# Writing out the second edge loop of a two-layer graph network on one Trainium2 core

## The reference

```python
h = gelu(edge_scalar_attr @ W_mlp1 / sqrt(8));  h = gelu(h @ W_mlp2 / sqrt(64))
w00, w01, w10, w11 = h @ Wp_00, h @ Wp_01, h @ Wp_10, h @ Wp_11
e0, e1 = feat0[edge_src], feat1[edge_src]          # a gather of 128 floats per edge
mid0 = [w00 * e0 * ea0,  w11 * sum(e1 * ea1) / sqrt(3)]
mid1 = [(w01 * e0) * ea1, w10 * e1 * ea0]
n0, n1 = segment_sum(mid0, edge_dst), segment_sum(mid1, edge_dst)
```

## Time and profile before

| | us |
|---|---|
| runs of the kernel | 5851.09, 5867.39, 5890.79 (median 5867.39) |
| span of the profiled execution | 5855.7 |
| edge loop of the second layer, first gather to last accumulation | 3144 to 5792 |
| busy in the span | PE 3865.5 (66%), DVE 3222.6 (55%), POOL 3371.9 (58%), ACT 1837.0 (31%) |

### The profile page before, as it was taken

How to read it: one execution, slowest core, us unless ns; L and a number is a source line. 1 busy time by engine, 2 the same in 40 slices (tenths; PEclk the granted TensorE clock), 3 DMA queues, 4 the chain that set the end, 5 groups by cost and what they waited for, 6 DMA issues and landing times. The chain is left out here.

```text
span 5855.7 us, 86247 instructions
## 1 busy us (share of the span) xinstructions
PE 3865.5 (66%) x15016; PEld 2606.4 (45%) x15016; DVE 3222.6 (55%) x10018; ACT 1837.0 (31%) x5130; POOL 3371.9 (58%) x3264
## 2 busy tenths in 40 slices
PE   2666666666666666666664775786776677776676
PEld 2334444434444444444443554554554455454454
DVE  3344454545444554454554675675666556675665
ACT  1234334344334344334452221221222122222221
POOL 3455555555555555555525776666777666767763
PEclk6878878888888888888876897887888778887787
DMA  5433333333333333333311111111111111111111
GB/s 151 120 103 100 100 99 98 93 101 104 96 100 100 100 98 101 98 102 99 101 51 54 44 44 43 43 42 43 44 43 44 41 42 44 44 42 45 43 42 41
DMA packets 395313, 430.82 MB, mean 74 GB/s; under 512 B 195187, under 2 KB 286839, under 8 KB 394888
## 3 DMA queue, kind: packets, MB, share of 16 engines
q0 software_dynamic: 103168, 211.49, 13.8%
q1 hardware_dynamic: 291560, 216.64, 13.7%
q10 hardware_dynamic: 288, 0.04, 0.0%
HBM read 411.18 MB, written 16.65 MB: 73 GB/s over the span
## 5 line engine op out<-in xcount | busy, mean ns | idle before, releaser
L171 POOL DMA_INDIRECT ring_rows<-xl,ring_idx x1612 | 1537.0, 953 | 1444.3 <-DVE attn_msg L1043 898.6
L218 POOL DMA_INDIRECT ahead_rows<-feat,ahead_idx x1612 | 1796.1, 1114 | 834.1 <-issue 513.5
L878 PE MATMUL attn_sums_ps<-attn_msg,attn_onehot 128*128 128x136 f32 x3224 | 601.9, 344 | 934.8 <-DVE c_acc_attn L984 541.8
L1433 PE MATMUL conv_sums_ps<-conv_vals,conv_onehot 128*128 128x256 f32 x3224 | 924.6, 436 | 157.6 <-issue 95.9
L878 PEld LDWEIGHTS attn_sums_ps<-attn_msg,attn_onehot 128*128 128x128 f32 x3224 | 524.3, 240 | 987.6 <-DVE c_acc_attn L984 742.6
L1464 ACT ACTIVATE conv_scaled<-conv_w_ps,c_xT 128x64 f32<-128x64 f32 x1612 | 373.4, 314 | 1643.7 <-remote 729.0
L1433 PEld LDWEIGHTS conv_sums_ps<-conv_vals,conv_onehot 128*128 128x128 f32 x3224 | 654.5, 214 | 414.1 <-issue 310.1
L1440 PE MATMUL conv_w_ps<-c_Wp,conv_hid 128*128 128x256 f32 x1612 | 505.7, 444 | 484.1 <-ACT conv_hid L1470 266.5
L929 ACT ACTIVATE attn_fifth<-attn_pre_ps,c_b_r 128x512 f32<-128x512 f32 x403 | 275.0, 683 | 1505.4 <-remote 953.7
L1049 DVE SCALAR_TENSOR_TENSOR attn_leaky<-attn_pre_ps,c_b_r,attn_fifth 128x512 f32<-128x512 f32 x403 | 301.1, 747 | 743.5 <-ACT attn_fifth L929 599.1
L1489 DVE TENSOR_SCALAR conv_onehot<-c_iota,c_dst_pos 128x128 f32<-128x128 f32 x1612 | 357.1, 297 | 509.0 <-remote 374.6
(11 more groups left out here) (214 smaller groups left out, 4795.7 us busy)
## 6 DMA issues: line engine op xcount, KB each, us to landing
c_xT<-in_attrT SPq DMA_DIRECT2D x403, 256.0 KB
attn_rel<-rel_group SPq DMA_DIRECT2D x403, 126.0 KB
ring_rows<-xl,ring_idx POOLq DMA_INDIRECT x1612
ahead_rows<-feat,ahead_idx POOLq DMA_INDIRECT x1612
ahead_radial<-in_radialT SPq DMA_DIRECT2D x806, 8.0 KB
attn_xr_win<-xr_parts SPq DMA_DIRECT2D x403, 31.5 KB
attn_limit<-limit SPq DMA_DIRECT2D x403, 16.0 KB
ahead_idx<-in_src_tiles SPq DMA_DIRECT2D x403, 2.0 KB
```

Of the source, the lines that this page charges most:

```text
L171: pool.indirect_dma_start(self.rows[:, b, t, :], None, self.q["xl"][:, :], bass.IndirectOffsetOnAxis(ap=self.idx[:, s.slot(2), j * TG + t: ...
L218: pool.indirect_dma_start(self.rows[:, k.slot(U), t, :], None, self.q["feat"][:, :], bass.IndirectOffsetOnAxis(ap=self.idx[b][:, t:t + 1], ...
L878: last = nc.tensor.matmul(to, onehot[:, g.slot(2), t, :], msg[:, g.slot(2), t, :, :].rearrange("p h o -> p (h o)"), start=wins > 1 or t == ...
L1433: last = nc.tensor.matmul(to, onehot[:, g.slot(2), t, :], vals[:, g.slot(2), t, :], start=wins > 1 or t == 0, stop=wins > 1 or t == TG - 1)
```

## The change

`steps` gets a flag `written_out`. With it, the middle part is not a `Fori` but a Python loop over the same turns, so that all 403 groups stand in the program one after the other. `Step` now carries `turns`, which says whether it belongs to that middle part, since its `i` may now be a plain number there; `index` and `uses` then give plain numbers. The five engines of `convolution` get the flag (PE and DVE in the variant that runs here). The attention and the short loops keep theirs.

```diff
 class Step:
-    def __init__(self, at, i=0, stride=U):
-        self.at, self.i, self.stride = at, i, stride
+    def __init__(self, at, i=0, stride=U, turns=False):
+        self.at, self.i, self.stride, self.turns = at, i, stride, turns
...
     def index(self, scale=1, plus=0):
         base = self.at * scale + plus
-        return base if isinstance(self.i, int) else self.i * (self.stride * scale) + base
+        return self.i * (self.stride * scale) + base if self.turns else base
...
-def steps(eng, total, peel, unroll, tail, body, last=0):
+def steps(eng, total, peel, unroll, tail, body, last=0, written_out=False):
...
-    if total - last > peel:
-        with eng.Fori(0, (total - last - peel) // unroll) as i:
+    turns = (total - last - peel) // unroll
+    if written_out:
+        for i in range(turns):
             for u in range(unroll):
-                body(Step(peel + u, i, unroll), lambda lag: True)
+                body(Step(peel + u, i, unroll, True), lambda lag: True)
+    elif turns > 0:
+        with eng.Fori(0, turns) as i:
+            for u in range(unroll):
+                body(Step(peel + u, i, unroll, True), lambda lag: True)
...
 # convolution: sync, gpsimd, scalar
-            steps(sp, G, PEEL, U, 0, body)
+            steps(sp, G, PEEL, U, 0, body, written_out=True)
-            steps(pool, G, PEEL, U, 0, body)
+            steps(pool, G, PEEL, U, 0, body, written_out=True)
-            steps(act, G, PEEL, U, TAIL, body)
+            steps(act, G, PEEL, U, TAIL, body, written_out=True)
 # convolution: tensor, vector
-                steps(pe, G, PEEL, U, TAIL, body)
+                steps(pe, G, PEEL, U, TAIL, body, written_out=wins == 1)
-                steps(dve, G, PEEL, U, TAIL, body)
+                steps(dve, G, PEEL, U, TAIL, body, written_out=wins == 1)
```

More of the change, by code:

```diff
@@ L57 @@
 class Step:
-    def __init__(self, at, i=0, stride=U):
-        self.at, self.i, self.stride = at, i, stride
+    def __init__(self, at, i=0, stride=U, turns=False):
+        self.at, self.i, self.stride, self.turns = at, i, stride, turns
     def back(self, n):
-        return Step(self.at - n, self.i, self.stride)
+        return Step(self.at - n, self.i, self.stride, self.turns)
     def index(self, scale=1, plus=0):
         base = self.at * scale + plus
-        return base if isinstance(self.i, int) else self.i * (self.stride * scale) + base
+        return self.i * (self.stride * scale) + base if self.turns else base
     def uses(self, n=1, by=1):
         base = (self.at // n + 1) * by
-        return base if isinstance(self.i, int) else self.i * (self.stride // n * by) + base
+        return self.i * (self.stride // n * by) + base if self.turns else base
     def slot(self, n):
@@ L225, in place @@
     s, j = WHERE[g.at]
-    return Step(s, g.i, SPAN // B), j, SIZES[s]
+    return Step(s, g.i, SPAN // B, g.turns), j, SIZES[s]
 def lines_in_slot(s):
     base = 16 * SAME_SLOT[s.at]
-    return base if isinstance(s.i, int) else s.i * (16 * B) + base
+    return s.i * (16 * B) + base if s.turns else base
 def messages(k, later, live):
-    if not isinstance(k.i, int):
+    if k.turns:
         return [k.back(STEADY + later)]
@@ L572, in one_slot @@
         def one_slot(g):
-            return not isinstance(g.i, int) or LOOP_FROM - STEADY - 2 <= g.at < G - AFTER_LOOP - STEADY - 1
+            return g.turns or LOOP_FROM - STEADY - 2 <= g.at < G - AFTER_LOOP - STEADY - 1
         def sums_slot(g):
@@ L601, in job_of @@
         def job_of(k):
-            return Step(0, k.i, 1)
+            return Step(0, k.i, 1, True)
         def job_nodes(table, job):
@@ L806, in body @@
                                  .partition_broadcast(H).rearrange("p a n -> p (a n)")).then_inc(limit_loaded[s.slot(2)], 16)
-                    if wins == 1 and not isinstance(k.i, int):
+                    if wins == 1 and k.turns:
                         job_on_sp(sp, job_of(k), k.at - PEEL)
@@ L823, in body @@
             def body(k, live):
-                if not live(0) or (isinstance(k.i, int) and k.at < EARLY):
+                if not live(0) or (not k.turns and k.at < EARLY):
                     return
-                if not isinstance(k.i, int) or k.at >= NX:
+                if k.turns or k.at >= NX:
                     pool.wait_ge(msg_ready, k.back(NX).uses())
@@ L893, in body @@
                         nc.tensor.transpose(turn_ps[:, s.slot(2), DROPS:DROPS + H], drop_row[:, :], ident[0:H, 0:H]).then_inc(max_turns, 1)
-                    if wins == 1 and isinstance(k.i, int) and k.at == G + 3:
+                    if wins == 1 and not k.turns and k.at == G + 3:
                         pe.sem_inc(hidden_ready, FC * JOBS)
-                    if not isinstance(k.i, int):
+                    if k.turns:
                         u, c = k.at - PEEL, k.at - PEEL - U_HIDDEN
@@ L1128, in body @@
                     sp.dma_start(x_rows[:, k.slot(4), :, :], nodes("x_pad", k)).then_inc(x_loaded[k.slot(4)], 16)
-                if isinstance(k.i, int) and k.at == 3:
+                if not k.turns and k.at == 3:
                     for n in range(CONV_ND):
@@ L1402, in body @@
             def body(k, live):
-                if not live(0) or (isinstance(k.i, int) and k.at < ND):
+                if not live(0) or (not k.turns and k.at < ND):
                     return
@@ L1413, in body @@
             def body(k, live):
-                if not live(0) or (isinstance(k.i, int) and k.at < AHEAD):
+                if not live(0) or (not k.turns and k.at < AHEAD):
                     return
-                if not isinstance(k.i, int) or k.at >= NX:
+                if k.turns or k.at >= NX:
                     pool.wait_ge(vals_ready, k.back(NX).uses())
```

6 lines of the change are left out of this document (3 added, 3 removed).

## The result

The kernel before takes 5871.5 us (median of 20 runs), the changed one 5892.8 us (20 runs): ratio 1.0041, 95% interval 1.0025 to 1.0057. The forecast was 5680 us. The saving of 188 us didn't come; the change made the kernel 21 us slower, 0.4%, which is small but clear of the noise.

A forecast was written before the change was run, and what follows sets the result against it. POOL was taken to set the end, through gathers, their stretching and the index wait. Savings of 148 + 40 = 188 us took the span from 5855.7 to 5668, plus 11.7 gives 5680 us; range over the cases 5330 to 5890.

The forecast's parts named there:

- The index wait, 148 us: POOL's 296 us wait for SP's index loads: half, 148 us, goes with the register instructions; bounds all or none.
- Stretched gathers, -40 us: POOL's gathers lengthened by DVE's work, 267 us: 40 us taken off because shorter slow stretches leave less lead to eat up.
- The turns, 0 of 8 us: 49 loop turns cost DVE 8 us; none counted, as POOL sets the end; the skill's fetch rule would give 146 us.
- Fetched code, 0: Instruction fetch for the written-out groups, costed as DMA traffic at nothing.
- Rival C: Slower: fetching the written-out code stops DVE, 180 us; 6050 us if slow stretches stay too; chance 0.15.
- B: Nothing measurable: register instructions only suffer from the slow stretches' cause; 5867 us, less 8 at best; chance 0.25.
- A: Floor reached: fewer instructions end the slow stretches, DVE follows POOL at 5.04 us per group; 5370 us; chance 0.20.
- what would show it: Signs: register rows gone, POOL's index wait about 150 us; wrong above all if slow stretches keep length and DVE's pace.

The follow-up runs named there:

- e1: Written-out kernel with a deeper ring (13 slots of gathered rows instead of 8, 8 of indices and radial values instead of 4): 5903.7 us, ratio 1.0079.
- e3: Written-out kernel with only the first two of each group's four gathers from group 8 on: 4852.3 us, ratio 0.828 to the kernel before.
- e4: Written-out kernel with three more unread products per group on DVE: 5853.2 us, ratio 0.9973 to the kernel before.
- e10: The changed kernel, unedited, on a chip of the second kind: 4355.1 us, ratio 1.0088 to the kernel before.
- e13: Changed kernel with DVE's part put back in the loop, the other four engines written out, on the first chip: ratio 1.0012 to the kernel before.
- e2: Written-out kernel with two more unread matmuls per group on TensorE: 5924.7 us, ratio 1.0126 to the kernel before.
- e5: Written-out kernel with a memset that POOL waits for behind every gather, on the second kind of chip: ratio 1.1410 to the kernel before.

## Why the prediction was wrong

*The index wait, 148 us: the step that failed.* "There SP handles 10 instructions in 13.3 us, 1.33 each; with 3 left at the same pace it is 4.0 us per group", and "I take half". The reading was right for the stretch shown: SP handled its ten instructions one by one there and waited for nothing. But with the 3 left, SP needs 25 us from one index load to the next in a slow stretch: it is no longer slow at instructions and stands at the radial load instead, behind TensorE, 889.5 us for something the profile can't name where the earlier trace rows had 306.1. I had that wait as the reason why none of the 296 us could go, and still took half. The index wait grew by 60 us, and in e1 105 us less of it gives no time: the gathers are 102 us longer. The account of the earlier trace rows closes, but a closed account says where POOL's time lies, not that it can be had.

*Stretched gathers, -40 us: the wrong sign.* On the first chip all 1612 gathers together are busy 1807.0 us where they were 1796.1, 11 more; on the second kind it is 26 us more, which is the loss. I named the bound "as much again below nothing" and didn't take it. I had shorter slow stretches shorten the gathers; e3 and e4 show that a busier DVE lengthens them (means of 1682 and 1237 ns), and e10 that it is enough to move DVE's row against them. The Trainium skill (SBUF — State Buffer, SBUF: two separate sides) says that descriptors of a DMA issued by GpSimd can't be written while DVE, in a mode that uses both of its ports, holds the port pair that the two share. The traces agree in that a gather takes 0.94 us beside a waiting DVE and 2.59 under a row of products; the port itself shows in no run.

*The turns, 0 of 8 us:* nothing speaks against it, though no run takes the turns away alone. *Fetched code, 0:* right. 170 packets came in between 3250 and 5770 and the DMA share stayed at 0.18; e13, with four engines written out, has a ratio of 1.0012. Rival C, which wanted 180 us, is refuted: the losses are 21 and 33 us, and in e10 DVE idles on issue for 0.2 us. By the rule of the Trainium skill (Runtime: NRT & Kernel Launch, Instruction fetch mechanics), priced as in the prediction, 146 us would have gone with the turns; the kernel got slower.

*The rivals.* B came closest: the slow stretches don't need the register instructions, for they stay when these go, now with longer stops of TensorE, and POOL's wait doesn't shrink. It didn't move to `vals_ready`, though; it is still for the indices, and what changed is why SP is late with them. That the instructions suffer from the same cause, as B had it, is not shown (L1500 above). Its evidence was in the earlier trace rows: written-out attention groups were hardly faster. I gave it 0.25 and the forecast 0.40, because one trace showed slow registers and slow stretches together. A needed the slow stretches to end with the instructions, and they didn't. Its state, DVE following POOL at 5.04 us per group, does exist: it is the whole stage on the second kind of chip, and there the change has nothing to win.

*Against "what would show it":* the register rows went, and "slow stretches keep both their length and DVE's 17 us per group" is what came, with 27.7 us for the first group (DVE's products from 3646.84 to 3674.50). The range, up to 5890, missed the median by 3 us; its upper end was B's time without a loss of its own, so that the miss is narrow says nothing for the sum: the forecast of 5680 is off by 213 us.

What stays open: why TensorE's results come late on the first chip, and only there, and why SP and DVE are slow at instructions there in a loop. In this stage lateness of 10 us and more goes when half of the gathers go (e3 against the changed kernel). It is not the number of sequencer instructions (the changed kernel), the lateness stays with more work on TensorE (e2) and with more on DVE (e4), and the clock was up when the product shown was issued. Paced gathers, gathers of half the bytes and loads without gathers were not tried on that chip. The Trainium skill's page on SBUF (same section) says that PE never waits for another engine at its port, so by that rule a port isn't the cause; no run here settles it.

## What to carry to other kernels

When an engine's own instructions look slow in the same stretches in which other engines' results come late, price the change once as if those instructions held the others up and once as if they didn't, and look for a row that tells the two apart (here and the earlier trace rows). Where POOL issues gathers back to back, DVE's instructions that touch SBUF alone lie under them: code that makes DVE busier, or only moves its row by 0.2 us, can lengthen the gathers, and when POOL sets the end that is the only effect left. In a loop where a busy DVE slows POOL and a waiting DVE frees it, a wait that is removed in one place comes back in another, so test it with a deeper and a shallower ring before counting on it.

## What was not expected of the hardware

- The same kernel takes 5776 to 5869 us on one chip and 4320 us on three others. The difference is in both stages: the edge loop begins at 3144 us on the first and at 2205 us on the second kind, and takes 2617 us and 2020 us from the first to the last start of L1516, DVE's first product of a group.
- On the first chip a result of TensorE can reach the engine that waits for it 36 us after its matmul was issued, while 20 gathers start in 24 us at 0.94 us each; on the others the same pace of gathers leaves TensorE at 76 matmuls in 24 us and the clock at 1.00.
- Register instructions with a median of 57 ns reached 1424 ns on the first chip and 71 ns on another, in the same program. On the first chip they were slow only on SP and DVE, and only in a loop: ACT's reached 80 ns, and what DVE kept in the written-out loop took 321 ns at most.
- A gather that starts under DVE's one-hots takes 1.00 us, one that starts under its accumulations 0.94, on the second kind of chip (means in e10), though DVE is busy in both.
- A memset of 0.22 us that POOL waits for behind every gather costs more than its length: from gather to gather it is 0.97 + 0.22 + 0.46 = 1.65 us instead of 0.96 + 0.31 = 1.27, so 0.38 x 1612 = 610 us, the whole difference of e5 (4930 against 4321).
